# Two adaLN layers on one core: up units of the experts in the attention's accumulator banks

## The chip, the cores and the metric

The kernel runs on one core of a Trainium2 chip. The metric is the device time of one execution in microseconds. The core has five engines that matter here, each working through its own list of instructions in order: TensorE (PE in the rows, its weight loads PEld), VectorE (DVE), ScalarE (ACT), GpSimd (POOL) and SyncE (SP), which issues the transfers. Matmuls write into an accumulator memory of eight banks, each of 512 float32 values per partition; VectorE and ScalarE read them there. Engines wait for each other by semaphores.

## The reference

Input x is 8 batches of 512 tokens with 128 features. Two layers follow one another; each has an attention part and a feed-forward part, both behind a layer norm with a per-batch shift and scale ("modulation").

```python
x = x + ga * L0_attn(layernorm(x) * (1 + ca) + sa)      # 16 heads of 8, rotary, softmax over 512 keys
x = x + gb * L0_ffn(layernorm(x) * (1 + cb) + sb)       # 8 experts of width 256, top 2:
#     layer_mult = silu(x @ w0[e]) * (x @ w1[e]);  sum over e of weight[e] * (layer_mult @ wo[e])
x = x + ga1 * L1_attn(layernorm(x) * (1 + ca1) + sa1)   # gated unit over q, k statistics
x = x + gb1 * L1_ffn(layernorm(x) * (1 + cb1) + sb1)    # one expert (512 wide, gelu) per batch
```

All eight experts are computed for all tokens; a token's weight is zero for six of them.

## The kernel before

Each batch goes through four stages: P (norm, projections of q, k and v, rotary, splitting q and k into three bf16 parts which go through DRAM into "stacks"), A (layer 0's attention), B (layer 0's experts), C (layer 1). The stages of different batches overlap: while batch b is in B, batch b+1 is in A, batch b-1 in C, and batch b+3 or so in P.

**The order.** No scheduler runs on the chip. A table, `SLOTS`, gives for every engine and every step of every batch a number, and `order_of(engine)` sorts the steps by it; `walk` (L543) then emits them. The table was made by a planner outside the file.

**Attention (A).** For each of 4 groups of heads there are 8 steps "max" and 8 steps "exp". A max step (`smax`, L918 on TensorE) writes 128 queries x 1024 scores into the pair of banks `scores_for_max` (`sm`); VectorE reduces them to maxima (L1557). GpSimd splits the maxima (`mparts`, L1905), TensorE transposes them (`mT`), ScalarE copies them out (`mrow`), and SyncE stores them as rows into `qs`, where they are subtracted as part of the next scores. An exp step (`sexp`, L945) writes scores with keys on the partitions into the pair `scores` (`se`), and ScalarE takes the exponential (L1269). `pvm` multiplies these with the values. Each step waits until the last use of its pair has been read: max for `a_max`, exp for `a_exp`. In batch 0, group 0, the max steps alternate between both pairs.

**Experts (B).** There are 16 units per batch, two halves of each of 8 experts. For unit u the "gate" step `w0` (L996) writes `hb @ w0` into the bank `expert_units` (`wp`) with three matmuls of split operands (L572, L573, L574, float32 in two parts); ScalarE takes the tanh (L1311), VectorE the first product (th + 1) * w0 (L1692, signal `b_u`). The "up" step `w1` (L1010) then writes `hb @ w1` into the same bank, and VectorE multiplies it in (L1698, signal `b_mu`). So the up unit waits for `b_u`, and the next gate unit for `b_mu`. `down` (L1024) multiplies the product with the third weight. In the last batch (7) the units have two banks of `se` and two of `sm`, since attention is over.

**The start.** Batch 0's first steps compete with the set-up: the modulation's columns (`mod_columns`, L854) and rows (`mod_rows`, L866, then `mod_second` on VectorE, L1475), the attention weights' transposes (`turn_weights`), and the split of the experts' weights into high and low halves (`e0_high`, `e1_high` on ScalarE, `e0_low` on VectorE, `e1_low` L1844 on GpSimd).

**Bank bookkeeping.** `M0_USES` and `M1_USES` list the steps that use the banks `shared_ab` and `shared_pc`, each with the signal that frees it. `bank_waits` (L550) looks up the use before a step in TensorE's order, and `bank_free` waits for it. `elsewhere` (L335) names the steps that use another bank in the last batch.

## Time and profile before

| | us |
|---|---|
| median of 3 runs | 1085.66 |
| lowest, highest | 1082.01, 1087.82 |
| the profiled execution | 1092.12 |
| its span, first to last instruction | 1089.9 |
| TensorE busy in it | 926.0 |
| VectorE busy | 776.2 |
| ScalarE busy | 655.6 |
| GpSimd busy | 426.8 |

Spans, busy times and waits are of the one profiled execution. "Busy" counts instructions of an engine in work, not what it waits for; a matmul's record includes some time in which it overlaps its neighbour, so a busy TensorE is not a TensorE at its peak. The granted clock is the mean of TensorE's two levels, 1.2 GHz and 2.4 GHz, as a share of the higher.

### The profile page before, as it was taken

Reading aid. Unit: us, or ns where it says so; the run is one execution under the profiler, and the core shown is the slowest. Engines: PE = TensorE matmul, PEld = TensorE weight load, DVE = VectorE, ACT = ScalarE, POOL = GpSimd, SP = SyncE. Lnnn points to the kernel's source line nnn. Section 1 sums busy time; section 2 is a strip of 40 time slices with the busy share of each in tenths; the row PEclk is TensorE's granted clock in tenths of the full one; section 3 lists DMA queues with packets and bytes.
Section 4 is the critical chain, followed back from the end, with each engine's and each line's share of the span. In section 5 each row is a group of like instructions: output and inputs, shape, how many; then the busy total and the mean of one; then the engine's idle time right before and its main releaser. Section 6 shows DMA issues by size and latency. Waiting matters only on the chain. (4 is left out here: it accounts for less than half of the span.)

```text
span 1089.9 us, 15616 instructions
## 1 busy us (share of the span) xinstructions
PE 926.0 (85%) x5176; PEld 513.5 (47%) x5176; DVE 776.2 (71%) x1467; ACT 655.6 (60%) x1176; POOL 426.8 (39%) x537
## 2 busy tenths in 40 slices
PE   4247678997899799998999998999998999889785
PEld 2111135443444355554554654446464466368553
DVE  6566678677756877788867777888878765546665
ACT  1236664666656758668768576866856756745441
POOL 2161042226112815574134364653556244454300
PEclk9558988999999989999999999999999899979876
DMA  8520304001300140111300014150001000010010
GB/s 233 154 66 30 60 30 98 33 1 55 59 2 1 32 101 9 34 43 58 62 1 13 16 61 86 59 105 11 1 25 33 2 21 16 20 35 1 18 34 10
DMA packets 54536, 47.09 MB, mean 43 GB/s; under 512 B 12393, under 2 KB 50025, under 8 KB 53114
## 3 DMA queue, kind: packets, MB, share of 16 engines
q1 hardware_dynamic: 53898, 45.85, 16.7%
q8 instruction: 42, 0.69, 0.3%
q14 instruction: 36, 0.29, 0.1%
q10 hardware_dynamic: 560, 0.26, 0.1%
HBM read 30.97 MB, written 14.73 MB: 42 GB/s over the span
## 5 line engine op out<-in xcount | busy, mean ns | idle before, releaser
L1557 DVE TENSOR_REDUCE negmax<-scores_for_max 128x2 f32<-128x1024 f32 x252 | 307.9, 1222 | 73.7 <-PE scores_for_max L932 71.3
L1269 ACT ACTIVATE probs<-scores 128x1024 f32<-128x1024 f32 x256 | 262.0, 1023 | 91.8 <-PE scores L956 90.7
L1030 PE MATMUL shared_ab<-eo,mu 128*128 128x128 f32 x1024 | 143.4, 283 | 9.0 <-ACT scaled L1383 4.8
L1030 PEld LDWEIGHTS shared_ab<-eo,mu 128*128 128x128 f32 x1024 | 129.0, 193 | 45.2 <-issue 28.1
L966 PE MATMUL weighted_values<-probs,vaug 128*32 128x512 f32 x1024 | 142.3, 630 | 1.0 <-ACT probs L1269 0.9
L1953 POOL TENSOR_TENSOR acc<-acc,scaled 128x512 f32<-128x512 f32 x55 | 71.2, 1294 | 178.8 <-ACT scaled L1383 178.7
L1692 DVE SCALAR_TENSOR_TENSOR mu<-th,expert_units 128x512 f32<-128x512 f32 x112 | 76.7, 685 | 72.4 <-ACT th L1311 71.6
L932 PE MATMUL scores_for_max<-ks,qs 48*128 48x512 bf16 x504 | 102.6, 404 | 27.8 <-DVE negmax L1557 19.4
L572 PE MATMUL expert_units<-hb_hi,e_lo 128*128 128x512 f32 x224 | 112.2, 501 | 15.3 <-DVE mu L1692 9.7
L956 PE MATMUL scores<-qs,ks 51*128 51x512 bf16 x512 | 102.2, 396 | 20.8 <-ACT probs L1269 17.7
L1311 ACT ACTIVATE th<-expert_units 128x512 f32<-128x512 f32 x112 | 66.8, 597 | 78.8 <-PE expert_units L574 77.2
L1698 DVE TENSOR_TENSOR mu<-mu,expert_units 128x512 f32<-128x512 f32 x112 | 76.5, 683 | 31.1 <-PE expert_units L574 30.5
L1383 ACT ACTIVATE scaled<-shared_ab,pick 128x128 f32<-128x128 f32 x220 | 68.5, 365 | 44.8 <-PE shared_ab L1030 41.4
L573 PE MATMUL expert_units<-hb_lo,e_hi 128*128 128x512 f32 x224 | 89.9, 402 | 0.0
L574 PE MATMUL expert_units<-hb_hi,e_hi 128*128 128x512 f32 x224 | 89.6, 400 | 0.0
L572 PEld LDWEIGHTS expert_units<-hb_hi,e_lo 128*128 128x128 f32 x224 | 42.6, 190 | 87.2 <-DVE mu L1698 28.6
L932 PEld LDWEIGHTS scores_for_max<-ks,qs 48*128 48x128 bf16 x504 | 24.6, 94 | 111.8 <-DVE negmax L1557 70.9
L956 PEld LDWEIGHTS scores<-qs,ks 51*128 51x128 bf16 x512 | 25.0, 94 | 88.2 <-ACT probs L1269 47.6
L1909 POOL CAST mpart<-negmax 128x16 bf16<-128x16 f32 x32 | 8.8, 274 | 142.0 <-DVE negmax L1557 141.9
L574 PEld LDWEIGHTS expert_units<-hb_hi,e_hi 128*128 128x128 f32 x224 | 42.9, 192 | 10.1
L573 PEld LDWEIGHTS expert_units<-hb_lo,e_hi 128*128 128x128 f32 x224 | 43.3, 193 | 0.9 <-issue 0.5
L1139 PE MATMUL shared_pc<-xdn,w 128*128 128x512 f32 x56 | 32.1, 657 | 9.4 <-ACT u L1366 8.9
(320 smaller groups left out, 1590.8 us busy)
## 6 DMA issues: line engine op xcount, KB each, us to landing
parts_d<-parts SPq DMA_DIRECT2D x15, 384.0 KB, 2.5
qs<-parts_d SPq DMA_DIRECT2D x14, 384.0 KB, 6.1
ks<-parts_d SPq DMA_DIRECT2D x14, 384.0 KB, 9.8
w<-in_L_ffn_w SPq DMA_DIRECT2D x16, 256.0 KB, 3.9
parts_d<-parts SPq DMA_DIRECT2D x15, 256.0 KB, 2.7
xp<-in_L_attn_x SPq DMA_DIRECT2D x8, 256.0 KB, 3.0
probs<-in_L_ffn_w_kernel SPq DMA_DIRECT2D x2, 1024.0 KB, 7.7
x<-in_L_attn_x SPq DMA_DIRECT2D x8, 256.0 KB, 2.9
```

The lines of the kernel that those rows point to most:

```text
L572: nc.tensor.matmul(out_ap, w_lo, x_hi, start=True, stop=False)
L573: nc.tensor.matmul(out_ap, w_hi, x_lo, start=False, stop=False)
L574: return nc.tensor.matmul(out_ap, w_hi, x_hi, start=False, stop=True)
L932: last = nc.tensor.matmul(max_bank(b, g, n)[:, 512 * m:512 * (m + 1)], qs[at, b % 2, p, t * P:(t + 1) * P], ks[at, b % 2, p, :], start=Tru ...
L956: last = nc.tensor.matmul(se[:, 512 * m:512 * (m + 1)], ks[at, b % 2, p, kt * P:(kt + 1) * P], qs[at, b % 2, p, :], start=True, stop=True)
L966: last = nc.tensor.matmul(pv[32 * j:32 * j + 32, :], vaug[:, kt, PAIRS * (j // 2) + GP * g + j % 2, :], probs[:, kt % 2, j % 2, j // 2, :] ...
L1030: last = nc.tensor.matmul(m0[:, at], mu[:, (2 * e + f) % 4, at], eo[:, e, f, :], start=(f == 0), stop=(f == HALVES - 1))
L1269: nc.scalar.activation(probs[:, kt % 2, j, :, :].rearrange("p m s -> p (m s)"), se[:, :], ACT.Exp)\
L1557: V.tensor_reduce(negmax[:, g % 2, :, n], max_bank(b, g, n)[:, :].rearrange("p (m s) -> p m s", m=2), AX, ALU.max, negate=True)\
L1692: V.scalar_tensor_tensor(out=mu[:, u % 4, :], in0=th[:, u % 2, :], scalar=1.0, in1=w0p(b, u), op0=ALU.add, op1=ALU.mult).then_inc(sig["b_u ...
L1698: V.tensor_tensor(mu[:, u % 4, :], mu[:, u % 4, :], w1p(b, u), ALU.mult).then_inc(sig["b_mu"], 1)
L1953: G.tensor_tensor(acc[:, :, :], acc[:, :, :], scaled[:, :, :], ALU.add).then_inc(sig["b_acc"], 1)
```

## The change

Up units no longer write `expert_units`. Units with odd u write the first bank of the maxima's pair, those with even u the first bank of the exponential scores' pair. Two new lists of uses make the waits: a max step or an odd up unit waits for whatever used `sm` last in TensorE's order, an exp step or an even up unit for what used `se` last. A gate unit waits only for the first product (`b_u`) of the gate unit before it, since the up unit is no longer in its bank. The last batch keeps its banks, and its first units also wait for batch 6's last product. The second column matmul waits until the first columns are copied out. All rows of `SLOTS` are new; every engine has the same steps as before in another order.

```diff
-    ("B", "w1"): dict(pe=(196, 202, 209, 216, 224, 231, 239, 245, 252, 259, 265, 278, 285, 294, 301, 310, 349, 359,
+    ("B", "w1"): dict(pe=(198, 203, 206, 220, 222, 232, 239, 246, 248, 258, 264, 277, 282, 295, 302, 310, 350, 364,
...
+MAX_USES = {("A", "max"): ("a_max", lambda g, n: 8 * g + n + 1, lambda g, n: True),
+            ("B", "w1"): ("b_mu", lambda u: u + 1, lambda u: u % 2 == 1)}
+EXP_USES = {("A", "exp"): ("a_exp", lambda g, kt, j: 8 * g + 2 * kt + j + 1, lambda g, kt, j: True),
+            ("B", "w1"): ("b_mu", lambda u: u + 1, lambda u: u % 2 == 0)}
...
 def elsewhere(stage, step, b):
 
-    return b == LAST and stage == "C" and step in IN_OTHER_BANKS
+    if (stage, step) == ("A", "max"):
+        return b == 0
+    return b == LAST and (stage == "C" and step in IN_OTHER_BANKS or (stage, step) == ("B", "w1"))
...
+def in_bank(uses, stage, step, args):
+
+    return (stage, step) in uses and (len(uses[stage, step]) < 3 or uses[stage, step][2](*args))
...
-            order = [u for u in order_of("pe") if u[:2] in uses and not elsewhere(u[0], u[1], u[3])]
+            order = [u for u in order_of("pe") if in_bank(uses, u[0], u[1], u[2]) and not elsewhere(u[0], u[1], u[3])]
...
         def w1p(b, u):
 
-            return sm[:, 512 * (u % 2):512 * (u % 2 + 1)] if b == LAST else wp[:, :]
+            if b == LAST:
+                return sm[:, 512 * (u % 2):512 * (u % 2 + 1)]
+            return (sm if in_bank(MAX_USES, "B", "w1", (u,)) else se)[:, 0:512]
...
                     if L:
                         pe.wait_ge(s_cr, 16 * N_CONST)
+                        pe.wait_ge(s_cols, 2)
...
+                elif b == 0:
+                    after(pe, "a_max", b, 8 * g + n)
                 else:
-                    after(pe, "a_max", b, 8 * g + n)
+                    if (g, n) == (0, 0):
+                        after(pe, "a_max", b, 0)
+                    bank_free(pe, MAX_USES, b, "A", "max", g, n)
...
-                after(pe, "a_exp", b, n)
+                bank_free(pe, EXP_USES, b, "A", "exp", g, kt, j)
...
                     if b == LAST:
                         after(pe, "a_exp", b, 32)
+                        after(pe, "b_mu", b, 0)
                 at = slice(u * P, (u + 1) * P)
-                if b == LAST:
-                    after(pe, "b_u", b, max(u - 1, 0))
-                else:
-                    after(pe, "b_mu", b, u)
+                after(pe, "b_u", b, max(u - 1, 0) if b == LAST else u)
...
                     if b == LAST:
                         after(pe, "a_max", b, 32)
+                        after(pe, "b_mu", b, 0)
+                    if b == 0:
+                        after(pe, "a_max", b, 32)
...
                 else:
-                    after(pe, "b_u", b, u + 1)
+                    for uses in (MAX_USES, EXP_USES):
+                        if in_bank(uses, "B", "w1", (u,)):
+                            bank_free(pe, uses, b, "B", "w1", u)
```

Three places show how the order moves. The first is TensorE in batch 1's units 2 and 3, while batch 2 is in attention. `e0` are gate weights, `e1` up weights; of a unit's three matmuls only the first is shown. L932 and L952 are max steps, L956 and L976 exp steps, L1030 and L1053 the down matmuls, L966 the values. Before:

```order
L572 MATMUL expert_units<-hb_hi,e0_lo 128x512
...
L932 MATMUL scores_for_max<-ks,qs 128x512 x2
L956 MATMUL scores<-qs,ks 128x512 x2
L1030 MATMUL shared_ab<-eo,mu 128x128 x4
L572 MATMUL expert_units<-hb_hi,e1_lo 128x512
...
L932 MATMUL scores_for_max<-ks,qs 128x512 x2
L572 MATMUL expert_units<-hb_hi,e0_lo 128x512
...
L956 MATMUL scores<-qs,ks 128x512 x2
L966 MATMUL weighted_values<-probs,vaug 32x512 x4
L572 MATMUL expert_units<-hb_hi,e1_lo 128x512
```

The change, from gate unit 2 too:

```order
L585 MATMUL expert_units<-hb_hi,e0_lo 128x512
...
L952 MATMUL scores_for_max<-ks,qs 128x512 x2
L976 MATMUL scores<-qs,ks 128x512 x2
L961 MATMUL shared_ab<-identb,mpart 48x128
L976 MATMUL scores<-qs,ks 128x512 x2
L585 MATMUL scores_for_max<-hb_hi,e1_lo 128x512
...
L585 MATMUL expert_units<-hb_hi,e0_lo 128x512
...
L952 MATMUL scores_for_max<-ks,qs 128x512 x2
L585 MATMUL scores<-hb_hi,e1_lo 128x512
```

The up unit between the two gate units is now that of unit 1 and writes the maxima's pair. Only the next gate unit stands between it and the next max step; the two exp steps have one small transpose between them.

The second place is TensorE's beginning: L889 and L905 transpose the input, L862 and L878 are the columns and L874 and L890 the rows of the modulation, L915 and L931 the value matmuls, L572 and L585 the first of a projection's three. Before:

```order
L862 MATMUL scores_for_max<-acc,kq 128x8 x6
L572 MATMUL shared_pc<-hp_hi,wp_lo 128x512
...
L874 MATMUL expert_units<-kq,acc 8x384
...
L915 MATMUL shared_pc<-wv,xp 128x128 x4
...
L932 MATMUL scores_for_max<-ks,qs 128x512 x2
L915 MATMUL shared_pc<-wv,xp 128x128 x4
L932 MATMUL scores<-ks,qs 128x512 x2
```

The change:

```order
L878 MATMUL scores_for_max<-acc,kq 128x8 x4
L866 MATMUL shared_ab<-ident,x1 128x128 x4
L878 MATMUL scores_for_max<-acc,kq 128x8 x2
L890 MATMUL expert_units<-kq,acc 8x384
...
L931 MATMUL shared_pc<-wv,xp 128x128 x4
L585 MATMUL shared_pc<-hp_hi,wp_lo 128x512
...
L952 MATMUL scores_for_max<-ks,qs 128x512 x2
L952 MATMUL scores<-ks,qs 128x512 x2
```

The modulation's rows and the value matmuls have moved ahead of the first projection, and all of batch 1's projections ahead of the first max step. The third place is GpSimd's beginning, with the low half of the up weights (`e1_lo`). Before:

```order
L1854 TENSOR_TENSOR rstd_p<-rstd_p,nhalf 128x4
L1858 TENSOR_SCALAR rstd_p<-mv_p 128x4
...
L1874 TENSOR_TENSOR hp_lo<-xp,hp_hi 128x512
L1883 TENSOR_TENSOR rem<-rot1,rot2 128x512
L1902 COPY vaug<-vtok 128x64x8
L1889 TENSOR_TENSOR rem<-rem,parts 128x512
L1895 TENSOR_TENSOR parts<-rem,parts 128x512
L1847 TENSOR_TENSOR e1_lo<-probs,e1_hi 128x2048
```

The change:

```order
L1877 TENSOR_TENSOR rstd_p<-rstd_p,nhalf 128x4
L1870 TENSOR_TENSOR e1_lo<-probs,e1_hi 128x2048
L1925 COPY vaug<-vtok 128x64x8
L1881 TENSOR_SCALAR rstd_p<-mv_p 128x4
...
L1897 TENSOR_TENSOR hp_lo<-xp,hp_hi 128x512
```

The long subtraction stood behind batch 1's parts and stands now ahead of batch 1's norm.

## Rows read from the trace of the kernel before

**Rows 1.** The page: its span and the busy time by engine

```profile
span 1089.9 us, 15616 instructions
...
PE 926.0 (85%) x5176; PEld 513.5 (47%) x5176; DVE 776.2 (71%) x1467; ACT 655.6 (60%) x1176; POOL 426.8 (39%) x537
```

**Rows 2.** Busy by window: stretch, length, engines, clock; last, reductions from 125 to 975

```profile
0.00:60.00 60.00, 20.26 (x64) 11.60 (x64) 34.42 (x82) 14.66 (x22) 17.31 (x15) 0.75 0.63 181
60.00:120.00 60.00, 36.84 (x204) 9.67 (x207) 41.29 (x47) 30.46 (x44) 17.38 (x28) 0.74 0.28 66
...
840.00:900.00 60.00, 57.16 (x308) 30.86 (x308) 42.84 (x88) 40.27 (x74) 21.34 (x26) 0.91 0.07 16
...
125.00:975.00 850.00, 776.71 (x4469) 426.54 (x4470) 625.89 (x1172) 562.95 (x1012) 360.74 (x464) 0.97 0.15 36
...
L1557 DVE TENSOR_REDUCE negmax<-scores_for_max 128x2 f32<-128x1024 f32 x223 | 272.4, 1221 | 57.2 <-PE scores_for_max L932 54.8 <-POOL mpart L1915 1.3
```

**Rows 3.** TensorE's waits from 125 to 975 us: total us, times, longest

```profile
PE scores L956 <- ACT probs L1269: 13.6, 26, 1.2
PE expert_units L572 <- DVE mu L1692: 9.7, 16, 3.5
PE scores_for_max L932 <- DVE negmax L1557: 9.6, 24, 1.1
...
PE expert_units L572 <- DVE mu L1698: 3.3, 10, 0.8
...
PE scores_for_max L932 <- ACT probs L1269: 1.3, 2, 1.1
```

**Rows 4.** Timeline of batch 1's units: start us, duration us, what, idle before

```profile
309.82 0.50 PE L572 MATMUL expert_units<-hb_hi,e_lo 128*128 128x512 f32 x1
...
312.19 0.50 PE L572 MATMUL expert_units<-hb_hi,e_lo 128*128 128x512 f32 x1 [0.52 <-DVE mu L1692]
...
313.09 0.39 PE L956 MATMUL scores<-qs,ks 51*128 51x512 bf16 x2
...
313.52 1.03 ACT L1269 ACTIVATE probs<-scores 128x1024 f32<-128x1024 f32 x1 [1.19 <-PE scores L956]
...
313.93 0.50 PE L572 MATMUL expert_units<-hb_hi,e_lo 128*128 128x512 f32 x1 [0.21 <-DVE mu L1698]
...
316.14 0.39 PE L932 MATMUL scores_for_max<-ks,qs 48*128 48x512 bf16 x2
...
317.86 0.39 PE L932 MATMUL scores_for_max<-ks,qs 48*128 48x512 bf16 x2 [0.24 <-DVE negmax L1557]
```

**Rows 5.** Timeline of the start, 19 to 80 us

```profile
19.38 1.45 PE L874 MATMUL expert_units<-kq,acc 128*8 128x384 f32 x2
...
23.80 0.55 DVE L1481 COPY mu<-expert_units 8x384 f32<-8x384 f32 x1 [1.43 <-PE scores L874]
...
30.62 0.41 DVE L1493 TENSOR_TENSOR mu<-th,scaled 8x256 f32<-8x256 f32 x1
...
38.03 0.69 DVE L1515 TENSOR_TENSOR vg<-rem,vg 128x512 bf16<-128x512 f32 x1 [0.70 <-ACT vg L1298]
...
43.93 0.80 SPq L755 DMA_DIRECT2D qs<-parts_d  x2
...
49.73 0.61 PE L932 MATMUL scores_for_max<-ks,qs 48*128 48x512 bf16 x2
...
60.29 4.60 POOL L1847 TENSOR_TENSOR e_lo<-probs,e_hi 128x2048 fp32r<-128x2048 f32 x1 [1.13 <-ACT e_hi L1201]
...
63.48 1.22 DVE L1557 TENSOR_REDUCE negmax<-scores 128x2 f32<-128x1024 f32 x1
...
68.64 1.11 PE L889 MATMUL shared_pc<-ident,xp 128*128 128x128 f32 x4 [4.41 <-ACT xp L1249]
...
72.61 1.22 DVE L1557 TENSOR_REDUCE negmax<-scores 128x2 f32<-128x1024 f32 x1
...
79.73 0.61 PE L956 MATMUL scores<-qs,ks 51*128 51x512 bf16 x2 [1.08 <-DMA qs<-mrow]
```

More of the change, by code:

```diff
@@ L294 @@
[L294 to L300 removed]
+    ("P", "load"): dict(sp=(9, 13, 24, 35, 46, 57, 80, 85)),
@@ new lines @@
+    ("A", "wog"): dict(dve=(248, 319, 398, 493, 573, 689, 740, 915)),
+    ("B", "load"): dict(sp=(19, 54, 64, 78, 89, 104, 118, 127)),
+    ("B", "oT"): dict(pe=(174, 324, 479, 634, 791, 946, 1109, 1255)),
+    ("B", "ot"): dict(act=(107, 193, 284, 390, 484, 591, 693, 797)),
+    ("B", "y"): dict(pe=(177, 330, 482, 637, 796, 950, 1113, 1256)),
+    ("B", "x1"): dict(dve=(269, 355, 440, 542, 633, 735, 841, 935)),
+    ("B", "stats"): dict(dve=(270, 357, 441, 543, 634, 741, 842, 938)),
+    ("B", "rstd"): dict(pool=(37, 64, 89, 128, 152, 193, 218, 247)),
@@ new lines @@
+    ("B", "xn"): dict(act=(113, 201, 289, 396, 493, 600, 698, 800)),
+    ("B", "xT"): dict(pe=(188, 339, 491, 650, 808, 968, 1122, 1261)),
+    ("B", "hT"): dict(act=(116, 204, 292, 399, 497, 602, 701, 803)),
+    ("B", "lo"): dict(pool=(40, 68, 92, 130, 153, 195, 222, 249)),
+    ("B", "gate"): dict(pe=(191, 343, 497, 655, 812, 972, 1126, 1263)),
+    ("B", "logits"): dict(dve=(277, 363, 447, 553, 643, 749, 849, 941)),
+    ("B", "top"): dict(dve=(278, 365, 450, 556, 649, 750, 851, 942)),
+    ("B", "route"): dict(act=(120, 210, 308, 409, 503, 607, 705, 805)),
@@ new lines @@
+    ("C", "out"): dict(pe=(539, 647, 885, 1012, 1119, 1228, 1306, 1335)),
+    ("C", "res"): dict(dve=(476, 548, 692, 774, 845, 917, 981, 1019)),
+    ("C", "stats3"): dict(dve=(477, 551, 693, 775, 846, 918, 982, 1020)),
+    ("C", "rstd3"): dict(pool=(103, 131, 170, 198, 223, 237, 263, 271)),
+    ("C", "xn3"): dict(act=(331, 412, 552, 634, 704, 776, 842, 846), dve=(15, 23, 24, 30, 31, 38, 53, 1021)),
+    ("C", "xT3"): dict(pe=(566, 768, 905, 1023, 1136, 1237, 1317, 1337)),
+    ("C", "nT3"): dict(act=(342, 471, 561, 638, 710, 779, 847, 864)),
@@ new lines @@
+    ("P", "wT"): dict(pe=(18, 24, 38, 40, 41, 44, 54, 56)),
+    ("P", "wsplit"): dict(dve=(88, 115, 120, 126, 175, 186, 187, 214)),
+    ("P", "colm"): dict(pe=(17, 19, 20, 21, 22, 25, 26, 27, 28, 30, 35, 37, 39, 42, 43, 55)),
+    ("P", "cols"): dict(dve=(73, 78, 79, 84, 93, 102, 108, 109, 112, 113, 114, 135, 147, 178, 188, 230)),
+    ("P", "modpe"): dict(pe=(23, 36, 45, 53, 57, 95, 111, 204)),
+    ("P", "raw"): dict(sp=(1, 2, 3, 4, 5, 6, 7, 8)),
+    ("P", "late"): dict(sp=(10, 11, 12, 17, 18, 25, 37, 43)),
```

251 lines of the change are left out of this document (110 added, 141 removed), and 176 rows, old and new, of the table SLOTS.

## The prediction

> **What bounds the kernel now.** I read the page first: TensorE is busy 85% of the span, VectorE 71%, ScalarE 60% [rows 1]. The windows then show that this is an average over two situations [rows 2]. From 125 to 975 us TensorE works 776.71 of 850.00 us; in the first 120 us it works 20.26 and 36.84 us of 60, at a granted clock of 0.75 and 0.74. So there are two stores of time: 73.3 us of TensorE idleness in the long middle, and 62.9 us in the first 120. The last 70 us are a chain of batch 7's own steps, which the change hardly touches.
>
> In the middle every engine takes its work in a fixed order, and TensorE waits where a bank of the accumulator memory is written again before its last reader is through. The list of its waits shows this [rows 3]: exponential scores behind ScalarE's exponential 13.6 us (26 times), an up unit behind VectorE's first product (L1692) 9.7 us (16), maxima's scores behind VectorE's reduction 9.6 us (24), a gate unit behind the second product (L1698) 3.3 us (10), maxima's scores behind an exponential 1.3 us (2). Together 37.5 us in 78 waits, half of all idleness there.
>
> How long one use holds a bank is in the timeline [rows 4]. A gate unit starts at 309.82, its up unit at 312.19: 2.37 us (three matmuls, tanh, product). The next gate unit starts at 313.93, so the up unit held the bank 1.74 us. A maxima use holds its pair from 316.14 to 317.86, 1.72 us. The exponential's use starts at 313.09 and the exponential is through at 313.52 + 1.03 = 314.55, 1.5 us.
>
> **Part 1, up units leave the gate units' bank.** The middle covers 223 of the 32 x 8 maxima reductions [rows 2], so about 7 batches, 122 us each. Held time per batch before: the expert bank 16 x (2.37 + 1.74) = 66 us, the maxima's pair 32 x 1.72 = 55 us, the scores' pair 32 x 1.5 = 48 us. After: expert bank 16 x 2.37 = 38 us; eight up units go to each pair, so 55 + 8 x 1.74 = 69 us and 48 + 14 = 62 us. The coupling inside a unit is gone (up to 13.0 us, the 9.7 and the 3.3), but one bank held for over half of the time has become two, and these two carry attention, which paces VectorE and ScalarE. No work is added: the same matmuls, tanh and products run, none longer. The pair's second bank stands empty while an up unit holds the first.
>
> What this does to the waits is a question of how close two uses of a bank stand in TensorE's order. I counted, from the end of batch 0's attention to the end of batch 6's units, the places where at most one other step stands between them. Before: 20 between exponential scores, 15 between maxima, 8 from a gate to its up unit, 26 from an up to the next gate unit, 69 in all. After: 33 and 20 in the same two chains, 6 from scores and 5 from maxima to an up unit, 10 and 16 from an up unit back to them, 1 between gate units, 91 in all. The stretches of order printed above show one of each kind. The trace has 37.5 us for the 69 places, 0.54 us each, and I take that price for the new ones: 22 x 0.54 = **+12 us**. Bounds: if the planner had spaced the new places so that nobody waits and the two unit waits go, -13 us; if each of the 22 cost the longest wait of an attention chain, 1.2 us [rows 3], +26 us. I take +12 because the kinds that grow are the very kinds that waited 50 times in the trace. Who waits behind a stalled TensorE: the second product and the expert's down matmuls, with slack, and the next exponential or reduction, with little.
>
> **Part 2, the start.** The new order is another in the first 80 us. Before [rows 5], the last part of batch 0's second stack was ready at 38.03 + 0.69 = 38.7, the stack loads were issued at 43.93 and the first maxima's scores ran at 49.73. Then came a jam: GpSimd was in the 4.60 us subtraction of the up weights from 60.29, batch 2's norm waited behind it, TensorE stood at batch 2's transposes until 68.64, the eighth reduction began at 72.61 and the first exponential scores at 79.73.
>
> After, the modulation's matmuls and rows (23.80 to 30.62 + 0.41 on VectorE, 7.2 us) stand ahead of the first projection, and the value matmuls too. The matmuls begin some 3 us before 19.38, so the rows end near 27.6; behind them come the lower part, projection, rotation, two rounds of parts with ScalarE, which in between has 1.9 us for gate weights and batch 1's norm and modulation. With the durations of before I get the last part at 47.8, 9 us later, and the first maxima's scores near 56.5, 7 us later. But the 4.60 us subtraction now stands at GpSimd's start, where that engine is idle, and batch 1's projections are over before the maxima. So eight reductions of 1.22 us run in a row, 9.8 us, done near 67. Split, transpose, row copy and load take from 72.61 + 1.22 = 73.83 to 79.73 before, 5.9 us, which gives 73: 7 us earlier. I take **-6 us**, since the steps behind may not be as quick to follow. Bounds: -10 if the stack is not late; +6 if the late stack is not caught up. The wait added to the second column matmuls (for VectorE's copies of the first) is under 0.4 us, behind the weights' transposes. The other added waits, on batch 6's last product and batch 0's last maxima, are for results long there: 0. Behind SyncE's load of batch 2's input, which waits for batch 1's projection inputs, now stands the stack: both are ready near 48, so nothing.
>
> **Part 3, the tail.** Batch 7 keeps its banks, and its steps change places only with neighbours. 0 us, bounds -3 and +3, four steps of 0.69 us (the part in [rows 5]) each way.
>
> **Sum.** 1092.12 (span 1089.9 and 2.2 around it) + 12 - 6 + 0 = 1098. This execution is 6.5 us above the median 1085.66; the same difference there gives **1092 us**.
>
> **A rule that speaks against the change.** In the rows the granted clock is 0.97 over the middle, and the window 840 to 900 has 0.91 [rows 2]: short stops are already there, and the clock falls in places. The Trainium skill, TensorE: Matmul & The Clock Gate, section A second HAM failure mode: psum-queue depth-cycling, says that many short stops of TensorE between groups of matmuls, while it cycles through accumulator banks, make the clock swing between its two levels. The trace agrees only faintly; the rival below prices it from rows.
>
> **The rivals.**
> Faster: the coupling inside the unit is what hurts. The gate units' chain (2.37 us instead of 4.11) lets units run ahead and TensorE always finds something; for it speaks VectorE's idleness before the first product, against it that TensorE itself waited only 13.0 us there. -13 - 6 = -19: 1067. It decides the case if the up unit's uses of the pairs fall where attention does not press.
> No change: the waits only change names; the middle's gain and loss nearly cancel and take the start with them: 1086, from 1081 to 1091. For it: no engine gets more work and TensorE is 91% busy in the middle. That is also what one would see if the banks were never the matter, so that the change in effect does nothing.
> Slower, start: the late stack is not caught up because batch 2's norm comes between again. +12 + 6: 1104.
> Slower, clock: more stops, and the middle runs at 0.91 instead of 0.97. 776.71 x (0.97/0.91 - 1) = 51 us: 1137 and more.
>
> **How the numbers follow.** Forecast 0.40 (own range 1087 to 1101); faster 0.26 (1060 to 1074); no change 0.23; late start 0.06; clock 0.05. The range 1065 to 1104 leaves out the clock, half of the late start and the lower part of the faster case, some 0.2. A measurement of this kernel can tell 0.5%, 5.4 us, from no change. Slower by more: both slow rivals and 0.7 of the forecast, 0.39. Faster by more: the faster rival and a sixth of the middle one, 0.30. Within: 0.31.
>
> **What would show it.** Right, if from 125 to 975 TensorE's idle time grows from 73 us towards 85, with new lines for an up unit waiting for a reduction or an exponential and for scores waiting for the second product, while the gate unit's waits for products fall under 2 us. The start is right if the first exponential scores run near 73. It is wrong if the waits of the exponential and maxima scores (24.5 us) do not grow, or if the middle's granted clock differs from 0.97 by over 0.02.

## The result, and the profile after

The changed kernel took **1120.13 us** in the median (1115.39 to 1121.50, three runs) against 1085.66: ratio **1.031**, 95% interval 1.026 to 1.036. On another chip, six runs against eleven of the kernel before gave 1.0289 (1.025 to 1.033). The prediction said 1092 and a range up to 1104, so it was wrong, by 28 us and in the direction that it held likeliest. The profiled execution took 1115.39 us. The page of its trace, to be laid beside [rows 1]:

```profile
span 1113.1 us, 15622 instructions
...
PE 932.4 (84%) x5176; PEld 516.1 (46%) x5176; DVE 786.4 (71%) x1467; ACT 654.8 (59%) x1176; POOL 423.1 (38%) x537
```

The windows of [rows 2] in the changed kernel (stretch, length, TensorE, its weight loads, VectorE, ScalarE, GpSimd, granted clock, DMA share, GB/s):

```profile
0.00:60.00 60.00, 18.19 (x58) 11.27 (x59) 37.15 (x76) 13.63 (x20) 18.86 (x14) 0.71 0.53 154
60.00:120.00 60.00, 38.96 (x196) 9.66 (x195) 41.28 (x53) 29.02 (x42) 15.44 (x29) 0.70 0.33 92
...
125.00:975.00 850.00, 763.56 (x4421) 415.92 (x4422) 620.71 (x1137) 555.48 (x998) 349.10 (x454) 0.97 0.14 35
```

And TensorE's waits from 125 to 975 us, to be laid beside [rows 3] (13 to 23 lines lie between the two kernels' line numbers):

```profile
PE scores L976 <- ACT probs L1292: 19.1, 27, 1.4
PE scores_for_max L952 <- DVE negmax L1580: 18.8, 29, 1.3
PE scores_for_max L585 <- DVE negmax L1580: 3.2, 9, 1.1
...
PE scores_for_max L952 <- DVE mu L1721: 3.1, 9, 0.7
```

From 125 to 975 us TensorE is now idle for 86.4 us instead of 73.3. The attention chains wait 37.9 us where they waited 23.2; up units behind a reduction (L585, 3.2 us) and scores behind the second product (L1721, 3.1) are the new lines.

**Where the time went.** Three events divide both traces: the first exponential of batch 0, that of batch 1, and the last product of batch 6's units. The stretch between the first two is batch 0's attention alone ("b0" in the tables); I call the next stretch the middle and the last one the tail. The rows are the windows of the two last stretches before the tail, first of the kernel before, then of the changed one:

```profile
80.40:141.60 61.20, 43.07 (x275) 9.84 (x274) 40.13 (x44) 38.24 (x46) 6.73 (x22) 0.91 0.20 43
141.60:938.30 796.70, 736.23 (x4261) 404.43 (x4259) 598.75 (x1108) 530.96 (x960) 339.26 (x436) 0.97 0.15 37
```

```profile
80.60:149.60 69.00, 49.01 (x277) 10.04 (x277) 43.14 (x50) 38.69 (x47) 7.95 (x23) 0.82 0.14 39
149.60:955.70 806.10, 732.73 (x4249) 405.61 (x4249) 597.44 (x1105) 529.71 (x959) 336.99 (x437) 0.98 0.15 36
```

All later tables use this division. Each row is from one trace; "clock" is the granted clock of batch 0's attention, and busy and idle are TensorE's.

| Kernel | first exp. | b0 attention | its clock | its busy | middle | idle in the middle | tail | span |
|---|---|---|---|---|---|---|---|---|
| before | 80.4 | 61.2 | 0.91 | 43.1 | 796.7 | 60.5 | 151.6 | 1089.9 |
| before, again | 79.5 | 63.2 | 0.88 | 45.1 | 789.8 | 57.2 | 151.3 | 1083.8 |
| changed | 80.6 | 69.0 | 0.82 | 49.0 | 806.1 | 73.4 | 157.4 | 1113.1 |
| changed, again | 81.4 | 66.1 | 0.87 | 46.1 | 801.9 | 73.9 | 157.1 | 1106.5 |

So the first exponential is not 7 us earlier but level, batch 0's attention takes 3 to 8 us more, the middle 5 to 16, the tail 6.

### The profile page after: what moved, and what is told of

Same layout as the page of the kernel before. It is cut to its first block and busy times, and to the rows that moved or that the text cites. A ratio compares the mean times of both kernels' runs of the same rounds, so it can differ in the third digit from the quotient of the medians.

```text
span 1113.1 us, 15622 instructions
## 1 busy us (share of the span) xinstructions
PE 932.4 (84%) x5176; PEld 516.1 (46%) x5176; DVE 786.4 (71%) x1467; ACT 654.8 (59%) x1176; POOL 423.1 (38%) x537
## 5 line engine op out<-in xcount | busy, mean ns | idle before, releaser
L1053 PE MATMUL shared_ab<-eo,mu 128*128 128x128 f32 x1024 | 143.3, 283 | 9.3 <-ACT scaled L1406 4.2
L1053 PEld LDWEIGHTS shared_ab<-eo,mu 128*128 128x128 f32 x1024 | 126.5, 191 | 46.5 <-issue 32.4
L952 PE MATMUL scores_for_max<-ks,qs 48*128 48x512 bf16 x504 | 104.1, 409 | 37.3 <-DVE negmax L1580 31.3
L976 PE MATMUL scores<-qs,ks 51*128 51x512 bf16 x512 | 103.4, 400 | 27.9 <-ACT probs L1292 23.3
L976 PEld LDWEIGHTS scores<-qs,ks 51*128 51x128 bf16 x512 | 25.3, 94 | 114.4 <-ACT probs L1292 56.2
L952 PEld LDWEIGHTS scores_for_max<-ks,qs 48*128 48x128 bf16 x504 | 24.6, 94 | 114.9 <-DVE negmax L1580 73.3
L1721 DVE TENSOR_TENSOR mu<-mu,scores_for_max 128x512 f32<-128x512 f32 x72 | 49.0, 684 | 27.1 <-PE scores_for_max L587 26.0
L585 PE MATMUL expert_units<-hb_hi,e_lo 128*128 128x512 f32 x112 | 55.2, 493 | 2.6 <-DVE mu L1715 1.9
L1721 DVE TENSOR_TENSOR mu<-mu,scores 128x512 f32<-128x512 f32 x56 | 38.2, 682 | 26.3 <-PE scores L587 26.1
L586 PE MATMUL expert_units<-hb_lo,e_hi 128*128 128x512 f32 x112 | 44.9, 401 | 0.0
L587 PE MATMUL expert_units<-hb_hi,e_hi 128*128 128x512 f32 x112 | 44.7, 399 | 0.0
L986 PEld LDWEIGHTS weighted_values<-probs,vaug 128*32 128x32 f32 x1024 | 20.7, 110 | 44.0 <-issue 36.1
L585 PE MATMUL scores<-hb_hi,e_lo 128*128 128x512 f32 x72 | 34.5, 479 | 4.9 <-DVE mu L1715 3.1
L585 PEld LDWEIGHTS expert_units<-hb_hi,e_lo 128*128 128x128 f32 x112 | 21.4, 191 | 36.2 <-issue 18.1
```

Of the source, the lines that this page charges most:

```text
L585: nc.tensor.matmul(out_ap, w_lo, x_hi, start=True, stop=False)
L952: last = nc.tensor.matmul(max_bank(b, g, n)[:, 512 * m:512 * (m + 1)], qs[at, b % 2, p, t * P:(t + 1) * P], ks[at, b % 2, p, :], start=Tru ...
L976: last = nc.tensor.matmul(se[:, 512 * m:512 * (m + 1)], ks[at, b % 2, p, kt * P:(kt + 1) * P], qs[at, b % 2, p, :], start=True, stop=True)
L986: last = nc.tensor.matmul(pv[32 * j:32 * j + 32, :], vaug[:, kt, PAIRS * (j // 2) + GP * g + j % 2, :], probs[:, kt % 2, j % 2, j // 2, :] ...
L1053: last = nc.tensor.matmul(m0[:, at], mu[:, (2 * e + f) % 4, at], eo[:, e, f, :], start=(f == 0), stop=(f == HALVES - 1))
L1721: V.tensor_tensor(mu[:, u % 4, :], mu[:, u % 4, :], w1p(b, u), ALU.mult).then_inc(sig["b_mu"], 1)
```

## The experiments

### Both kernels once more

> The kernel before, profiled a second time, because its first profiled execution (1092.12 us, span 1089.9) lay 6.5 us above its median and the changed kernel's (1115.39) 4.7 below its own. If the difference is the granted clock's play in the first 150 us, the milestones differ there and the middle (796.7) and tail (151.6) repeat within 2 us. If the middle is shorter too, near 792, then the middle's true growth is nearer 10 than 5 to 9 us.

> The changed kernel itself again, on the chip on which the three below run. Its profiled execution took 1115 us (span 1113.1), its three timed runs 1115 to 1121, against 1086 before. If the cause lies in the program alone (order and banks), the ratio comes out at 1.03 again, between 1.026 and 1.036, and its milestones as in the first profile: first exponential of batch 1 near 149.6 us, last product of batch 6's units near 955.7. If the granted clock of single executions plays the larger part, the ratio moves by over 0.5% or the first 150 us are another length than 149.6 by more than 3 us.

Measured: before 1085.75 (ratio 0.9999, 0.997 to 1.003), changed 1.0289. The traces are in the table. The middle of before was 789.8 this time: its idle time repeats within 3.3 us, and its busy time was 732.6 us at a clock of 0.98 against 736.2 at 0.97. In the eleven runs of the kernel before that stood beside the second measurement of the changed one, the span of the unchanged kernel goes from 1076.7 at a mean clock of 0.94 to 1088.3 at 0.923. One pair of traces can therefore not measure 10 us here: the first two spans lie 23.2 us apart, the medians 31 and 34.

### Banks without order, order without banks

The first kernel has the change's code with the table of before. Seventeen steps had to move, of this kind (VectorE):

```diff
+A max (2, 6), batch 1
 B w1 (3), batch 0
-A max (2, 6), batch 1
```

> Banks changed, order kept: the up units write the first bank of the maxima's or the exponential scores' pair, and every engine takes its steps in the order of before, except for 17 steps on VectorE and ScalarE that go 1 to 6 places earlier (an up unit now waits for a reduction or an exponential that stood behind the unit's own product). Counted as in the prediction, this order has 134 places where at most one other step stands between two uses of a bank, against 67 to 69 before and 91 in the changed kernel. Theory of close places (0.54 us each, from the trace of before): the middle (first exponential of batch 1 to last product of batch 6's units, 796.7 us before) grows by 65 x 0.54 = 35 us to 832, the start stays at 141.6 us, the span is near 1125. Rival, the coupling inside the unit was what cost: middle 784, span 1077. Rival, banks do not matter at all and only the order does: middle 797, span 1090.

The second has the code of before with the new table, units put back in turn in the places that the table gives them (TensorE, batch 4):

```diff
 B w0 0
 B w1 0
-B w1 1
 B w0 1
+B w1 1
 B w0 2
-B w0 3
 B w1 2
+B w0 3
```

> Order changed, banks kept: every engine takes its steps in the order of the changed kernel, but up units write the gate units' bank as before, so gate and up units have to alternate on TensorE and VectorE (202 of their places get another unit), and 14 steps on VectorE and ScalarE go 1 or 2 places earlier. It has 140 close places, 87 of them in the one expert bank. Theory of close places: the middle grows by about 71 x 0.54 = 38 us to 835, the start is that of the changed kernel (149.6), the tail too, so the span is near 835 + 149.6 + 157 = 1142. Rival, the new banks are what costs 9 us in the middle and the order is harmless: middle 797, span 1104.

Measured: **1233.27 us** (1.137, 1.132 to 1.143) and **1330.01 us** (1.228, 1.222 to 1.235). The middles took 935.4 and 1016.0 us, four and six times the loss that I had expected. TensorE's waits in the middle, new banks with the old order and then old banks with the new:

```profile
PE scores_for_max L585 <- DVE negmax L1580: 52.7, 44, 2.5
PE scores L585 <- ACT probs L1292: 43.1, 34, 3.5
PE scores_for_max L952 <- DVE mu L1721: 16.9, 24, 1.9
PE scores L976 <- DVE mu L1721: 14.7, 19, 1.4
```

```profile
PE expert_units L572 <- DVE mu L1698: 76.3, 70, 2.7
PE expert_units L572 <- DVE mu L1692: 49.6, 42, 2.5
```

Where an up unit waits behind attention's last use of a pair, it waits 1.2 us in the mean (95.8 us in 78 waits). Neither half of the change can be judged alone: the order is made for its banks. The price of 0.54 us per close place also falls. These two have 67 and 73 close places more than before and lost 138.7 and 219.3 us in the middle, 2.1 and 3.0 us for each. My reading, which no run tests apart, is that a close place costs what the order around it leaves it to cost.

The same runs bear on the rival of the clock. The windows of their middles:

```profile
145.10:1080.50 935.40, 768.53 (x4261) 418.98 (x4259) 601.85 (x1107) 533.79 (x960) 336.85 (x436) 0.94 0.13 31
```

```profile
152.30:1168.30 1016.00, 813.73 (x4249) 433.68 (x4249) 597.15 (x1106) 532.84 (x959) 336.41 (x437) 0.90 0.11 29
```

With 167 and 202 us of idleness instead of 60, the granted clock is 0.94 and 0.90 and the same matmuls are busy for 32 and 77 us more. With the 73 us of the changed kernel it is 0.98. By the Trainium skill, TensorE: Matmul & The Clock Gate, section A second HAM failure mode: psum-queue depth-cycling, frequent short stops between groups of matmuls make the clock swing; the lower mean clocks of these two middles agree, the changed kernel's middle does not show it.

### Wider spacing in TensorE's order

Thirty neighbours change places, of this kind (`x` is any step that does not use the pair):

```diff
 A exp, use n of the pair
 x
-A exp, use n + 1
 y
+A exp, use n + 1
```

> The changed kernel with 30 swaps of neighbours in TensorE's order between 150 and 956 us, and nothing else: where exponential scores (16) or maxima's scores (14) stood with at most one step behind the last use of their pair by the same kind, they change places with the step behind them. Close places of these two kinds fall from 52 to 25, all together from 91 to 60. In the trace the gaps ahead of such places are 0.57 us in the mean (18.3 us for 32 exponential, 11.3 for 20 maxima's), against 0.08 to 0.13 where more steps stand between. Theory of close places: the middle (802 to 808 us) gets 27 x 0.45 = 12 us shorter, 792 to 796, as long as in the kernel before, ratio 1.018. Rival, ScalarE's exponentials and VectorE's reductions set the pace there and the gap only moves to the next step: 802 to 808 again. Rival, the later scores delay exponentials that TensorE needs soon: longer.

Measured: 1121.46 us (1.032, 1.029 to 1.036). TensorE's waits in its middle:

```profile
PE scores_for_max L952 <- DVE negmax L1580: 15.5, 25, 1.8
PE scores L976 <- ACT probs L1292: 10.8, 17, 1.5
...
PE weighted_values L986 <- ACT probs L1292: 3.4, 6, 1.0
```

The scores wait 26.3 us instead of some 35, but the weighted values now wait 3.4 us behind exponentials instead of 0.5, and the idle time of the middle is 70.3 us, where the kernels with the unspaced middle have 70.8 to 75.5: at most 3 us gained where 12 were expected. With a clock of 0.96 the middle was even 813.0 us long. This fits the first rival of the run (the exponentials and reductions set the pace, and the gap moves to the next step), though its 802 to 808 us was not met.

### The start, and what follows it

> The changed kernel, but every engine first takes the steps that it had begun in the kernel before by 141.6 us (the first exponential of batch 1), in the order of before; the rest follows in the changed order. No unit of an expert stands in this part, so only the order is undone, not the banks. Theory (the start's loss is its order's): first exponential of batch 1 at 141.6 us instead of 149.6, middle (806) and tail (157) as in the changed kernel, span 1105, ratio to before 1.022 where the changed kernel has 1.030. Rival, the loss was handed on from the granted clock and not from the order: span 1113 again. Rival, the steps behind catch up or fall back: the 8 us appear but the middle grows by as much.

```diff
-every engine: changed order from the first step on
+every engine: the steps begun before 141.6 us in the kernel before, in its order
+every engine: all other steps, in the changed order
```

Measured: 1.0245 (1.021 to 1.028); first exponential at 80.6, batch 0's attention 60.6 us at 0.90, middle 805.9, tail 156.9. In the trace the start's loss is gone, as expected: batch 1's first exponential is at 141.2 us. In the medians 1.0289 less 1.0245 is 5 us, with intervals that overlap; the run with only the middle changed, below, settles start and tail together.

Why was the first exponential not early? The timeline of the changed kernel's start (start us, duration us, what, idle before), to be laid beside [rows 5]:

```profile
22.27 4.50 POOL L1870 TENSOR_TENSOR e_lo<-probs,e_hi 128x2048 fp32r<-128x2048 f32 x1 [13.44 <-ACT e_hi L1224]
22.38 5.14 DVE L1508 TENSOR_SCALAR mu<-mu 8x256 f32<-8x256 f32 x2
...
31.43 0.41 DVE L1516 TENSOR_TENSOR mu<-th,scaled 8x256 f32<-8x256 f32 x1
...
44.61 2.28 DVE L1548 TENSOR_TENSOR e_lo<-probs,e_hi 128x2048 fp32r<-128x2048 f32 x1
44.87 2.12 POOL L1883 TENSOR_SCALAR shift_p<-mv_p 128x4 f32<-128x4 f32 x1
...
53.33 1.35 DVE L1538 TENSOR_TENSOR vg<-rem,vg 128x512 bf16<-128x512 f32 x1 [2.02 <-ACT vg L1321]
...
62.44 0.61 PE L952 MATMUL scores_for_max<-ks,qs 48*128 48x512 bf16 x2 [1.16 <-DMA ks<-parts_d]
...
71.48 1.23 DVE L1580 TENSOR_REDUCE negmax<-scores 128x2 f32<-128x1024 f32 x1
```

Two 8 x 256 operations of the modulation take 5.14 us beside GpSimd's 4.50 us subtraction, against 0.60 in the kernel before. At 44.87 it is GpSimd's turn: a 128 x 4 operation, 0.23 us elsewhere in this trace, takes 2.12 beside VectorE's own 2.28 us subtraction, and ScalarE's batch 1 norm and, behind it, its part of batch 0 wait for that. The last part itself takes 1.35 us at 53.33, from 0.69 before [rows 5], beside another operation of GpSimd. The test moves the subtraction (`e1lo`), and lets two steps of GpSimd go ahead of the one behind it:

```diff
 P rstd, batch 0
-P e1lo, batch 0
 A vcopy, batch 0
...
 P split (1), batch 1
-C w2g, batch 0
-P lo, batch 2
+P e1lo, batch 0
 A mparts (0), batch 0
+P lo, batch 2
+C w2g, batch 0
```

> The changed kernel with one step moved on one engine: GpSimd takes the subtraction of the up weights' lower part (4.50 us from 22.27) behind batch 1's second split, where batch 0's reductions run on VectorE, and no longer beside VectorE's modulation rows; the batch 0 maxima's parts and batch 2's lower part go ahead of the w2 rows behind it. Theory (VectorE and GpSimd hold each other up): the two 8 x 256 operations of the modulation that took 5.14 us together fall back to 0.6 each or so, the rows end at 27.3 instead of 31.84, first maxima's scores at 58 instead of 62.4, first exponential at 76 instead of 80.6, span 4.5 us shorter than the changed kernel's (1106.5 to 1113.1), ratio 1.025. The reductions, which read accumulator memory, stay at 1.22 us beside the subtraction. Rival, the rows wait for something else (the column matmuls or a DMA): they end at 31.8 again and nothing is gained. Rival, the subtraction in its new place holds the maxima's parts up: first exponential again near 80.

```profile
22.61 0.60 DVE L1508 TENSOR_SCALAR mu<-mu 8x256 f32<-8x256 f32 x2
```

Measured: 0.60 us for the two, first maxima's scores at 58.42, first exponential at **75.8**, all as the theory said. The ratio, 1.0252 (1.021 to 1.029), is where the theory put it but not clear of the changed kernel's 1.0289, and in this trace the gain did not last: batch 1's first exponential came at 148.0. The stretch between took 72.2 us:

```profile
75.80:148.00 72.20, 53.70 (x277) 10.58 (x277) 43.10 (x50) 38.64 (x47) 7.93 (x23) 0.74 0.14 37
```

The same 277 matmuls were busy 53.70 us at 0.74 that took 43.07 at 0.91 (275) in the kernel before; the idle time beside them hardly differs, 18.5 and 18.1 us. Batch 0's attention is thus long in the traces in which the granted clock is low. The next kernels ask what goes with that.

> The kernel before, with the changed kernel's order up to 80.6 us (the first exponential) and the subtraction of the up weights' lower part moved as in the run above; everything behind in the order of before. Theory: eight reductions in a row without the jam behind the subtraction, and no collision on VectorE: first exponential at 76 instead of 80.4, then the 61 us to batch 1's first exponential as before, so 137 instead of 141.6, middle and tail unchanged, ratio to before 0.996. Rival, the 61 us become 66 to 69 as in the changed kernel (the attention of batch 0 is slower whenever it starts behind eight ready maxima): ratio 1.001 to 1.003. Rival, the steps that the old order had by then and the new not (second split of batch 1 among them) are met later and cost the 4 us back: ratio 1.000.

> The changed kernel with the order of before only up to the first exponential (80.4 us); from there the changed order. With the old order on both sides of 80 us the stretch to batch 1's first exponential took 60.6 to 66.1 us (clock 0.91, 0.88, 0.90, 0.81), with the new on both sides 66.1 to 73.5 (0.87, 0.82, 0.80, 0.77, 0.71), with the new before and the old behind 69.5 (0.74). If the order before 80 us decides over the clock behind it, this run has 61 to 64 us at 0.88 or more. If the order behind it decides, 66 to 70 at 0.8.

> The kernel before with one step moved on GpSimd: the 4.60 us subtraction of the up weights' lower part goes from 60.29 us behind the first group's maxima's parts (73.9). The prediction read a jam behind it: batch 2's norm, TensorE at batch 2's transposes until 68.64, eighth reduction at 72.61, first exponential at 80.4. Theory: norm at 60.3 instead of 64.97, eighth reduction at 68, first exponential at 76. Then either the 61 us to batch 1's first exponential stay (first exponential of batch 1 at 137, ratio 0.996), or the granted clock takes the gain back as in the two runs that began early (69.5 and 72.2 us at 0.74): 142 to 146, ratio 1.00. After those runs I expect the second.

The first two change from one order to the other at 80 us as their texts say; the third moves one step on GpSimd in the kernel before:

```diff
 P split3 (0), batch 1
-P e1lo, batch 0
 P rstd, batch 2
...
 A mparts (0), batch 0
+P e1lo, batch 0
```

| Kernel | first exp. | b0 attention | clock | middle | tail | ratio |
|---|---|---|---|---|---|---|
| new order to 80, old behind, subtraction late | 76.8 | 69.5 | 0.74 | 786.2 | 152.7 | 0.998 (0.995 to 1.001) |
| changed kernel, old order to 80 | 78.9 | 72.1 | 0.74 | 806.3 | 155.6 | 1.026 (1.022 to 1.030) |
| before, subtraction later | 78.9 | 67.2 | 0.77 | 791.0 | 151.4 | 1.001 (0.998 to 1.003) |

The second goes against "the order before 80 us decides": old order there, yet 72.1 us at 0.74. The third had a surprise at 70.84 us (timeline, VectorE, then GpSimd):

```profile
70.84 5.75 DVE L1520 TENSOR_TENSOR wh_lo<-otok,wh_hi 128x512 fp32r<-128x512 f32 x1
...
69.79 4.62 POOL L1847 TENSOR_TENSOR e_lo<-probs,e_hi 128x2048 fp32r<-128x2048 f32 x1
74.34 1.28 POOL L1935 TENSOR_TENSOR w<-w,cgb 128x512 f32<-128x512 f32 x1
```

Its eighth reduction ran at 67.49 instead of 72.61, so the prediction's jam was real; but the subtraction, in its new place, held up another of VectorE's (0.75 us in the kernel before), and the first exponential came at 78.9.

Does added work raise the clock? One line in the exponential scores' step, in three kernels:

```diff
                 last.then_inc(sig["a_sef"], 1)
+                if b == 0:
+                    nc.tensor.matmul(wp[:, :], ks[at, 0, p, kt * P:(kt + 1) * P], qs[at, 0, p, :], start=True, stop=True)
```

> The changed kernel with one more matmul behind each of batch 0's 32 exponential scores: the same operands, 128 x 512, into the expert units' bank, which is empty there; nobody reads it. It is work without use, meant only to keep TensorE busier between 80 and 150 us. In the traces so far that stretch is always 17 to 20 us of TensorE idleness plus its busy time, and the busy time goes with the granted clock: 43.1 us at 0.91, 45.1 at 0.88, 46.1 at 0.87, 49.0 at 0.82, 52.0 at 0.74. Theory (the clock, not the order, makes this stretch 66 to 69 us in the changed kernel): it rises to 0.95 or more, the stretch takes 60 us at most, the 6.8 us of added matmuls go into the idle time, and the span gets 7 us shorter, 1104. Rival, the clock is not moved by TensorE's load: the stretch stays at 66 to 69 us or grows by the 7 us added.

> The same 32 added matmuls in the kernel before. Its stretch from the first exponential of batch 0 to that of batch 1 was 61.2 and 63.2 us at 0.91 and 0.88. Theory: 59 to 60 us at a clock of 0.95 or more, ratio to before 0.998. Rival: the added matmuls fall between scores that are waited for, 64 us or more, ratio 1.002.

> The kernel before with the changed kernel's order up to the first exponential, the up weights' subtraction behind batch 1's splits (first exponential at 76.8 us in the run above, but then 69.5 us at a clock of 0.74), and the 32 added matmuls. If the clock took the 3 to 4 us back, then with it at 0.95 the first exponential of batch 1 is at 137 us instead of 141.6 to 146.3, and the ratio to before is 0.993 to 0.996. If not, 146 again and a ratio of 0.998.

Measured: 67.0 us at 0.89 (ratio 1.028, 1.023 to 1.032), 64.0 at 0.89 (1.001, 0.999 to 1.004) and 62.2 at 0.93 (0.999, 0.997 to 1.002). Only in the last did the stretch get shorter, from 69.5 at 0.74, and its median did not (1084.49 us against 1082.95 without them). That added load raises the clock is not shown: 0.89 and 0.93 lie above all traces with any part of the new order (0.71 to 0.87), but 0.89 in the kernel before is no more than its 0.91 and 0.88 without them. Added matmuls, some 7 us of work, bring no time in any case.

### The tail, and the middle alone

> The changed kernel up to the last product of batch 6's units (955.7 us in its profile), the rest on every engine in the order of before; batch 7's banks are the same in both kernels. Theory (the tail's +5.8 is its order's: the expert weights of batch 7 stand ahead of the first two units' products on VectorE and beside GpSimd's four 1.28 us operations, and take 6.66 us instead of 2.92): the tail is 151.6 us again instead of 157.1 to 157.4, the weights take 3 us, the span is 5.5 us shorter than the changed kernel's. Rival, the tail is longer because it is entered with other work left over: 157 again.

> The changed kernel with one step moved on VectorE: batch 7's expert weights (nine small operations, 6.66 us from 991.04) go from ahead of the first unit's products to behind those of units 0 and 1, as in the kernel before. Theory: the first two units' tanh and products no longer wait for them (first product 6 us earlier); what comes back depends on whether the weights still run beside GpSimd's 1.28 us operations: tail 151.5 if they take 3 us, 155 if they take 6.7 again, against 157.2 and 157.4. Rival, the place doesn't matter since the first down matmul waits for the weights' readers anyway: 157.

> The changed kernel with the start of before (every step begun before 141.6 us) and the tail of before (every step behind 955.7 us of the changed kernel's profile); only the middle, 806 us of it, and with it the banks, is changed. The traces with one middle or the other give 784 to 797 us (five traces of the old one, mean 789.4) against 802 to 809 (six of the new, mean 805.5). Theory: the middle costs 16 us of the 31, and the other 15 are gone: first exponential of batch 1 at 141 to 143, tail 152, span near 1099, ratio to before 1.014 to 1.016. Rival, the middle's length hangs on what the start hands over: 790 us, ratio 1.00; or all three losses come back in another place: ratio 1.025.

The second moves one step on VectorE:

```diff
-B weights, batch 7
 B w0 (0), batch 7
...
 B w1 (1), batch 7
+B weights, batch 7
```

Measured: old tail 1.024 (1.019 to 1.029), its tail 152.1 us; weights later 1.027 (1.024 to 1.031), tail 155.7; middle alone **1.017** (1.0145 to 1.020), 62.7 us for batch 0's attention at 0.91, middle 810.2, tail 154.1. The middle alone is clear of the changed kernel's 1.029 (1.025 to 1.033): start and tail together cost 1.2%, some 13 us. One by one their gains of 5 us have intervals that overlap with it, and rest on the traces. The order of before takes the tail from 157 to 152.1 us, and to 154.1 in the run with only the middle changed. That the weights are its cause is not shown: with them moved, the first product came 5 to 6 us earlier in the tail, but the tail was only 1.5 us shorter, and traces with the weights unmoved have 154.3 (the changed kernel with added matmuls) to 157.7. They still took 5.2 us there. In the changed kernel they took 6.66, for this reason (VectorE, then GpSimd):

```profile
992.63 1.16 DVE L1699 TENSOR_TENSOR pick<-iota,pick 128x32 f32<-128x32 f32 x1
993.71 1.31 DVE L1700 TENSOR_TENSOR pick<-iota,pick 128x32 f32<-128x32 f32 x1
995.05 1.20 DVE L1701 TENSOR_TENSOR pick<-pick,pw 128x32 f32<-128x32 f32 x1
...
992.44 1.30 POOL L660 TENSOR_TENSOR kq<-qz,gam 128x512 f32<-128x512 f32 x1
993.70 1.27 POOL L662 TENSOR_TENSOR kq<-kq,bet 128x512 f32<-128x512 f32 x1
994.93 1.27 POOL L664 TENSOR_TENSOR kq<-kq,bet 128x512 f32<-128x512 f32 x1
```

Each small operation ends 0.05 us behind one of GpSimd's. In the kernel before, where GpSimd was through at 978.49, the same operation takes 0.19 us:

```profile
978.63 0.19 DVE L1676 TENSOR_TENSOR pick<-iota,pick 128x32 f32<-128x32 f32 x1
```

The middle repeats well. Nine traces of kernels with the new one give 801.9 to 810.2 us (mean 806.5, idle 70.8 to 75.5), eight with the old one 784.3 to 796.7 (mean 790.2, idle 56.5 to 62.3): 16 us, of which 14 are idleness. TensorE's waits account for them. In the first two traces, from 141.6 to 938.3 and from 149.6 to 955.7 us, the waits of maxima's and exponential scores for their own kind went from 19.7 to 35.0 us, those between up units and scores in the shared pairs are new (9.7), and those inside the unit fell from 13.0 to 1.9: 13.9 us more in all, with 12.9 us more idleness. VectorE's and GpSimd's holding each other up is not in it: they are busy for 597.4 and 337.0 us in the changed middle, against 598.8 and 339.3.

The loss has its places: from batch 2's first exponential to batch 3's it is 98.6 and 98.8 us in the two traces of before and 104.2 in both of the changed kernel, from batch 4's to batch 5's 97.6 twice and 103.7 and 103.6; the other five intervals give and take. In the first of them stalls of exponential scores of up to 1.4 us are new (4.7 us in 5 waits, from 1.1 in 3), and one of 2.2 us at a transpose behind the copy of a maxima's row. What makes the new order dear in these places stays open.

### A version faster than both

Two steps in the kernel before: the subtraction as above, and on VectorE the one that it had held up:

```diff
 A max (1, 0), batch 0
-P whlo, batch 0
 A max (1, 1), batch 0
...
 P stats, batch 3
+P whlo, batch 0
```

> The kernel before with two steps moved: GpSimd's subtraction of the up weights' lower part behind the first maxima's parts, as in the last such run, and VectorE's subtraction of the hidden weights' lower part (two operands in the on-chip buffer, 128 x 512) behind batch 3's statistics, where GpSimd does only small work. In the last run that second one took 5.75 us from 70.84 beside GpSimd's 4.62 and 1.28, against 0.75 in the kernel before, and the first exponential came at 78.86 instead of 76. Theory: it takes 0.7 us, the first exponential is at 75 to 76; then, as in the three runs before, the clock takes the gain back: batch 1's first exponential at 142 to 147, ratio 1.000. Rival, the gain stays: 137, ratio 0.996.

> The same with the 32 added matmuls without use behind batch 0's exponential scores (128 x 512 into the empty expert units' bank). They gave 64.0, 62.2 and 67.0 us at clocks of 0.89, 0.93 and 0.89 where the stretch without them took 61 to 63, 69.5 and 66 to 69. Theory: 75.5 + 62.5 = 138 us for batch 1's first exponential against 141.6 and 142.7 before, ratio 0.996 to 0.998. Rival: as without them, 1.000.

```profile
76.28 0.68 DVE L1520 TENSOR_TENSOR wh_lo<-otok,wh_hi 128x512 fp32r<-128x512 f32 x1
```

Measured: **1082.57 us, 0.996 (0.994 to 0.998)**, and 1081.68, 0.997 (0.994 to 0.999) with the added matmuls. First exponential at 75.2, batch 0's attention 61.8 us at 0.91, batch 1's first exponential at 137.0. Here the rival was right and I was not: the gain stayed. It is small, 4 us, and the added matmuls add nothing to it (62.7 us at 0.93).

## Why the prediction was wrong, step by step

**The middle, +12: held roughly in size, not in its reasoning.** Idle time in 125 to 975 us went from 73.3 to 86.4 (85 was said), new lines of the kinds named appeared, a unit's waits behind the first product fell to 1.9 us and those of the gate units behind the second are gone, the clock stayed. Timed alone it is +19 us (1.017), inside the bounds of -13 and +26. But 0.54 us per close place is no price: it was 2.1 and 3.0 where the order did not fit the banks, and taking 27 places away brought at most 3 us of idleness and no time. What the count caught was which chains would wait more, attention's.

**The start, -6: the step that failed.** Batch 1's first exponential came 5 to 8 us later in the traces (149.6 and 147.5 against 141.6 and 142.7), and the run with the old start was 5 us faster. "With the durations of before I get the last part at 47.8": it was at 54.7. The subtraction was placed "at GpSimd's start, where that engine is idle", and what VectorE did there was not looked at. The durations did not move with the steps, because VectorE and GpSimd hold each other up: 4.5 us at the modulation's rows (shown by the run with the subtraction late), about 1.9 more at GpSimd's 128 x 4 operation and 0.7 at the last part itself (both read, not tried alone). The eight reductions did run in a row and ended at 72.7 instead of 67. And an early first exponential need not have been a gain: with the new order the 61 us behind it became 66 to 73 us, with the same matmuls at a lower clock. The prediction let the stretch behind the start count as unchanged.

**The tail, 0: the second step that failed.** It was put at nothing because "its steps change places only with neighbours", and it cost some 5 us, above the bound of 3; the order of before brings 3 to 5 us back. One such change put the expert weights ahead of the first unit's products and beside four operations of GpSimd, 6.66 us instead of 2.92. Moved back alone, they brought no more than 1.5, so which of the other steps cost the rest stays open.

**The sum and the range.** 19 for the middle, 5 and 5 for start and tail make 29 of the 31 to 34 us. The range took the terms one at a time: its end of 1104 is the late start, a middle at its own bound of +26 would have been 1106, and all three losses together lay outside it. Of the rivals, the one of the clock in the middle did not come. The late start came, by another cause than the one named: a held-up VectorE, not batch 2's norm. The faster one (decoupling) is not borne out: the unit's 13 us of waits fell to 1.9, and attention's grew by 15. Whether another order for the new banks could do better is open; only this one and a bad one were seen.

What sets the clock in batch 0's attention stays open too. Without added matmuls, the seven traces with the order of before on both sides of 80 us had 0.81 to 0.91 six times and 0.77 once (the subtraction moved), the nine with any part of the new order 0.71 to 0.87. Order goes with it, but the spread inside one order, 66.0 to 73.5 us for the same start and attention, is as large as the difference. A single trace of such a kernel says little about this stretch.

## What to carry to other kernels

When a change moves steps, look at what the other of VectorE and GpSimd does in the new place before using a duration of the old one: small operations there took the length of their neighbour's. A gain ahead of a stretch whose clock swings has to be read behind that stretch. And where an order is planned for its banks, a count of tight places told here which waits grow, not what one costs.

## What the hardware showed that was not expected

**VectorE and GpSimd hold each other up on some operations.** Beside a GpSimd operation of 1.27 to 4.62 us, VectorE's operations with two operands in the on-chip buffer (128 x 32: 0.19 to 1.16 and 1.31 us; 128 x 512: 0.75 to 5.75) and a one-operand 8 x 256 (0.60 for two to 5.14) ended only behind it. Reductions of accumulator memory kept their 1.22 us [rows 5, at 63.48 beside the subtraction from 60.29], and so did 128 x 512 operations with one operand there (0.69). The Trainium skill, SBUF — State Buffer, section Who interferes with whom, says that VectorE contends with GpSimd when it has two operands in the buffer or runs in a two-port mode, and of the latter that whoever issues first keeps the shared ports for the whole instruction. The rows above agree, save that the 5.75 us operation let a second one of GpSimd pass before it. The small operation of GpSimd beside VectorE (0.23 to 2.12 us) is the same in the other direction. But not every operation of GpSimd holds VectorE up for its whole length. In the changed kernel two of the weights' operations ran inside one of GpSimd's at their usual 0.19 and 0.18 us:

```profile
527.89 1.06 POOL L1886 TENSOR_TENSOR rstd_c<-rstd_c,nhalf 128x4 f32<-128x4 f32 x1
528.08 0.19 DVE L1701 TENSOR_TENSOR pick<-pick,pw 128x32 f32<-128x32 f32 x1
528.19 0.18 DVE L1703 TENSOR_TENSOR pick<-pick,pw 128x32 f32<-128x32 f32 x1
```

**The granted clock of batch 0's attention**, a stretch with 17 to 20 us of TensorE idleness in 61 to 73, lay anywhere from 0.71 to 0.91, a mixture of the levels 1.2 and 2.4 GHz, for 275 to 277 of the same matmuls. Its busy time went from 43.1 to 55.1 us with it, one per cent of this kernel.
